# Cross-attention and routed experts on one core: a second norm with its own statistics, its first tile earlier, and weight splits in halves

## What is computed

```
def _layernorm(x, axis=-1, eps=1e-05):
    m = jnp.mean(x, axis=axis, keepdims=True)
    v = jnp.var(x, axis=axis, keepdims=True)
    return (x - m) / jnp.sqrt(v + eps)
...
        scores = jnp.einsum('bhqd,bhkd->bhqk', q, k) / jnp.sqrt(jnp.float32(D_K))
        scores = jnp.where(m == 0, jnp.float32(NEG_INF), scores)
        p_attn = jax.nn.softmax(scores, axis=-1)
        x = jnp.einsum('bhqk,bhkd->bhqd', p_attn, v)
        return jnp.einsum('bsd,ed->bse', x, Wo) + bo
...
        xa = xf @ P_w.T
        C1 = _route_combine_weights(xa, U1, K_ROUTE, TAU)   # top 3 of 12, softmax over them
        h = jax.nn.gelu(_mixture(xf, C1, W1), approximate=False)
        y = _mixture(h, C2, W2) + C3 @ b2
...
    x = x + _L0_xattn_ref(_layernorm(x, axis=-1), ctx_1024, ctx_1024, mask_BxSxS2_ik1, ...)
    x = x + _L0_ffn_ref(_layernorm(x, axis=-1), ...)
```

## Time and profile before

| | us |
|---|---|
| median of 3 runs | 414.63 |
| lowest, highest | 414.23, 415.75 |
| span of the profiled execution | 412.4 |

### The profile page before, as it was taken

How to read it: one execution, slowest core, us unless ns; L and a number is a source line. 1 busy time by engine, 2 the same in 40 slices (tenths; PEclk the granted TensorE clock), 3 DMA queues, 4 the chain that set the end, 5 groups by cost and what they waited for, 6 DMA issues and landing times.

```text
span 412.4 us, 7824 instructions
## 1 busy us (share of the span) xinstructions
PE 392.4 (95%) x2132; PEld 331.0 (80%) x2132; DVE 342.9 (83%) x1036; ACT 115.8 (28%) x263; POOL 110.9 (27%) x165
## 2 busy tenths in 40 slices
PE   4499999999989999999999999999999999999996
PEld 4388988989868888888888888888888888888884
DVE  3998889889885889789897988989789898888875
ACT  3477888888822111010110101011010100101000
POOL 5462755657520220202112020211202112020200
PEclk9999999999989999999999999999999999999999
DMA  7900123131000000000000000000000000000000
GB/s 225 333 2 2 61 92 98 55 102 51 2 0 3 0 2 13 13 0 13 0 13 13 0 13 0 13 0 13 13 0 13 0 13 13 0 13 0 14 0 26
DMA packets 8612, 12.71 MB, mean 31 GB/s; under 512 B 1076, under 2 KB 5016, under 8 KB 8472
## 3 DMA queue, kind: packets, MB, share of 16 engines
q1 hardware_dynamic: 8040, 12.44, 9.1%
q10 hardware_dynamic: 560, 0.13, 0.1%
HBM read 10.47 MB, written 2.10 MB: 30 GB/s over the span
## 4 chain that ended last, share of the span: by engine, by line
PE 89%; DVE 4%; issue 3%; ACT 2%; DMA 1%; POOL 1%; ACTq 0%; DVEq 0%; POOLq 0%
PE banks L920 68%; PE banks L997 5%; PE banks L987 3%; PE banks L962 3%; PE banks L972 2%; PE banks L975 2%; PE banks L977 2%; PE banks L1035 1%; DMA bk_sb<-in_bk_dram 1%; PE banks L1043 1%; DVE q_hl L625 1%; PE banks L1025 1%; PE banks L1008 1%; PE banks L953 1%; DVE s_max L631 1%
## 5 line engine op out<-in xcount | busy, mean ns | idle before, releaser
L815 DVE SCALAR_TENSOR_TENSOR s_d<-banks,c_cur,s_d 128x256 f32<-128x256 f32 x165 | 72.7, 478 | 27.6 <-PE banks L920 23.1
L920 PE MATMUL banks<-w_h,xf_h 128*128 128x512 f32 x204 | 81.8, 401 | 0.0
L920 PE MATMUL banks<-w_l,xf_h 128*128 128x512 f32 x204 | 80.6, 395 | 0.0
L920 PE MATMUL banks<-w_h,xf_l 128*128 128x512 f32 x204 | 80.2, 393 | 0.0
L406 POOL TENSOR_TENSOR top_e<-euler,top_d 128x9 f32<-128x9 f32 x16 | 28.9, 1807 | 185.1 <-DVE top_d L765 185.1
L920 PE MATMUL banks<-w_h,h_h 128*128 128x512 f32 x180 | 73.5, 408 | 0.0
L920 PE MATMUL banks<-w_l,h_h 128*128 128x512 f32 x180 | 71.1, 395 | 0.0
L920 PE MATMUL banks<-w_h,h_l 128*128 128x512 f32 x180 | 71.1, 395 | 0.0
L815 DVE SCALAR_TENSOR_TENSOR sum<-banks,c_new,sum 128x256 f32<-128x256 f32 x160 | 66.6, 476 | 3.2 <-PE banks L920 3.1
L561 ACT ACTIVATE h_h<-banks 128x256 fp32r<-128x256 f32 x15 | 5.8, 385 | 156.5 <-PE banks L1043 156.5
L920 PEld LDWEIGHTS banks<-w_l,xf_h 128*128 128x128 f32 x204 | 38.6, 189 | 8.5
(11 more groups left out here) (126 smaller groups left out, 618.5 us busy)
## 6 DMA issues: line engine op xcount, KB each, us to landing
stage<-in_w_t_dram SPq DMA_DIRECT2D x12, 512.0 KB, 3.7
out_dram<-x_all SPq DMA_DIRECT2D x16, 128.0 KB, 1.9
x_all<-in_x_dram SPq DMA_DIRECT2D x1, 1024.0 KB, 8.0
x_all<-in_x_dram SPq DMA_DIRECT2D x1, 768.0 KB, 7.9
mask_all<-in_mask_dram SPq DMA_DIRECT2D x2, 256.0 KB, 5.1
x_all<-in_x_dram SPq DMA_DIRECT2D x2, 128.0 KB, 3.5
wk_sb<-in_wk_t_dram SPq DMA_DIRECT2D x1, 256.0 KB, 3.7
wq_sb<-in_wq_t_dram SPq DMA_DIRECT2D x1, 256.0 KB, 4.3
```

What stands on the lines that cost most here:

```text
L815: dve.scalar_tensor_tensor(out=sums[e % 2][:, :], in0=product, scalar=weights[:, e:e + 1], in1=sums[e % 2][:, :], op0=ALU.mult, op1=ALU.ad ...
L920: ins = pe.matmul(dst, a(c), b(c), start=(i == 0), stop=(i == len(terms) - 1))
```

## The change

It has four parts.

1. The second norm gets tiles of its own: `bn2`, `mean_var2`, `var_eps2`, `rstd2`, and functions of its own on VectorE (`stats2`, `normalise2`) and GpSimd (`inverse_deviation2`).
2. Its first tile moves. On VectorE the statistics of tile 0 stand ahead of step T-4 = 12 and its normalisation right behind that step; statistics of tile 1 stand behind `xf_low(0)`. On GpSimd the inverse deviation of tile 0 stands ahead of the split of chunk 10 (it stood ahead of that of chunk 11).
3. ScalarE rounds `xf_h` from PSUM, not from `xf_t`, and waits neither for its own copy nor for `xf_low` of the tile before; VectorE's `xf_low` subtracts from PSUM as well. What overwrites `ps_t` waits for `xf_lo` where it waited for `xf_copied` (TensorE's `transpose_xf(1)`, `transpose_h`).
4. GpSimd splits each weight chunk in two instructions of 128x512.

```
             def split_weights(n, slot):
                 pool.wait_ge(w_hi, n + 1)
-                pool.tensor_tensor(w_l[:, n, :, :], stage[:, slot, :, :], w_h[:, n, :, :].bitcast(F32),
-                                   ALU.subtract).then_inc(w_split, 1)
+                for c in range(C):
+                    ins = pool.tensor_tensor(w_l[:, n, c, :], stage[:, slot, c, :], w_h[:, n, c, :].bitcast(F32),
+                                             ALU.subtract)
+                ins.then_inc(w_split, 1)
...
                     add_output_bias(T - 1)
-                    inverse_deviation(0, stats2_ready, var2_ready, rstd2_ready)
+                if n == CHUNKS - 2:
+                    inverse_deviation2(0)
                 split_weights(n, n % RING)
...
                 if later(t, 1):
                     act.wait_ge(z_done, t)
-                    act.wait_ge(xf_lo, t)
                 nc.scalar.activation(xf_t[:, :, :], ps_t, ACT.Copy).then_inc(xf_copied, 1)
-                act.wait_ge(xf_copied, t + 1)
-                nc.scalar.activation(xf_h[:, :, :], xf_t[:, :, :], ACT.Copy).then_inc(xf_hi, 1)
+                nc.scalar.activation(xf_h[:, :, :], ps_t, ACT.Copy).then_inc(xf_hi, 1)
...
+            stats2(0)
             attention(T - 4)
-            statistics(0, x_all, bn2_done, stats2_ready)
+            normalise2(0)
 
             def xf_low(t):
+                dve.wait_ge(xf_copied, t + 1)
                 dve.wait_ge(xf_hi, t + 1)
-                dve.tensor_tensor(xf_l[:, :, :], xf_t[:, :, :], xf_h[:, :, :].bitcast(F32), ALU.subtract).then_inc(xf_lo, 1)
+                dve.tensor_tensor(xf_l[:, :, :], ps_t, xf_h[:, :, :].bitcast(F32), ALU.subtract).then_inc(xf_lo, 1)
...
             a_low(T - 4)
-            normalise(0, x_all, xf, rstd2_ready, xf_ready)
             q_low(T - 1)
             divide_by_sum(T - 3)
             add_attention(T - 4)
-            statistics(1, x_all, bn2_done, stats2_ready)
             xf_low(0)
+            stats2(1)
...
                 pe.wait_ge(xf_ready, t + 1)
                 if later(t, 2):
                     pe.wait_ge(h_lo, t - 1)
+                elif t == 1:
+                    pe.wait_ge(xf_lo, 1)
                 else:
-                    pe.wait_ge(xf_copied if t else xt_copied, 1 if t else T)
+                    pe.wait_ge(xt_copied, T)
...
             def transpose_h(t):
                 pe.wait_ge(h_ready, t + 1)
                 n = min(t + 2, T) if isinstance(t, int) else t + 2
-                pe.wait_ge(xf_copied, n)
+                pe.wait_ge(xf_lo, n)
```

More of the change, by code:

```diff
@@ L132, in xattn_ffn_kernel @@
         rstd = sb("rstd", [P, 1])
+        bn2 = sb("bn2", [P, 6])
+        mean_var2 = sb("mean_var2", [P, 2])
+        var_eps2 = sb("var_eps2", [P, 1])
+        rstd2 = sb("rstd2", [P, 1])
         xn = sb("xn", [P, D])
@@ L350, in _, with inverse_deviation, inverse_deviation2 @@
             pool.wait_ge(consts_set, 16)
-            def inverse_deviation(t, stats, var, out_sem):
-                pool.wait_ge(stats, t + 1)
-                pool.tensor_tensor(var_eps[:, :], mean_var[:, 1:2], eps[:, :], ALU.add).then_inc(var, 1)
-                pool.wait_ge(var, t + 1)
-                pool.tensor_tensor(rstd[:, :], var_eps[:, :], minus_half[:, :], ALU.pow).then_inc(out_sem, 1)
+            def inverse_deviation(t):
+                pool.wait_ge(stats_ready, t + 1)
+                pool.tensor_tensor(var_eps[:, :], mean_var[:, 1:2], eps[:, :], ALU.add).then_inc(var_ready, 1)
+                pool.wait_ge(var_ready, t + 1)
+                pool.tensor_tensor(rstd[:, :], var_eps[:, :], minus_half[:, :], ALU.pow).then_inc(rstd_ready, 1)
+            def inverse_deviation2(t):
+                pool.wait_ge(stats2_ready, t + 1)
+                pool.tensor_tensor(var_eps2[:, :], mean_var2[:, 1:2], eps[:, :], ALU.add).then_inc(var2_ready, 1)
+                pool.wait_ge(var2_ready, t + 1)
+                pool.tensor_tensor(rstd2[:, :], var_eps2[:, :], minus_half[:, :], ALU.pow).then_inc(rstd2_ready, 1)
             def add_output_bias(t):
@@ L365, in split_weights @@
                 pool.wait_ge(w_hi, n + 1)
[L366 to L367 removed]
+                for c in range(C):
+                    ins = pool.tensor_tensor(w_l[:, n, c, :], stage[:, slot, c, :], w_h[:, n, c, :].bitcast(F32),
+                                             ALU.subtract)
+                ins.then_inc(w_split, 1)
             def attention(t):
[L370 removed]
+                inverse_deviation(t)
                 add_output_bias(t - 1)
[L373 to L374 removed]
+            inverse_deviation(0)
+            inverse_deviation(1)
             pool.wait_ge(setup_dve, 5)
             place_low_keys(pool, 0, kbd_set)
[L377 removed]
+            inverse_deviation(2)
             pool.wait_ge(bo_in, 16)
@@ L425, in _ @@
             exponentials(0)
-            inverse_deviation(1, stats2_ready, var2_ready, rstd2_ready)
+            inverse_deviation2(1)
             exponentials(1)
@@ L429, in _ @@
             with pool.Fori(2, T) as t:
-                inverse_deviation(t, stats2_ready, var2_ready, rstd2_ready)
+                inverse_deviation2(t)
                 exponentials(t)
@@ L592, in _, with statistics, stats2 @@
         def _(dve):
-            def statistics(t, src, done, ready):
-                dve.bn_stats(bn[:, :], src[:, t, :]).then_inc(done, 1)
+            def statistics(t, parts, dst, done, ready):
+                dve.bn_stats(parts[:, :], x_all[:, t, :]).then_inc(done, 1)
                 dve.wait_ge(done, t + 1)
                 dve.memset(waited[:, :], 0.0)
-                dve.bn_aggr(mean_var[:, :], bn[:, :]).then_inc(ready, 1)
-            def normalise(t, src, dst, rstd_sem, ready):
-                dve.wait_ge(rstd_sem, t + 1)
-                dve.tensor_scalar(dst[:, :], src[:, t, :], mean_var[:, 0:1], rstd[:, 0:1],
-                                  ALU.subtract, ALU.mult).then_inc(ready, 1)
+                dve.bn_aggr(dst[:, :], parts[:, :]).then_inc(ready, 1)
             def stats1(t):
-                statistics(t, x_all, bn_done, stats_ready)
+                statistics(t, bn, mean_var, bn_done, stats_ready)
+            def stats2(t):
+                statistics(t, bn2, mean_var2, bn2_done, stats2_ready)
             def normalise1(t):
@@ L610, in normalise1 @@
                     dve.wait_ge(xt_done, t)
-                normalise(t, x_all, xn, rstd_ready, xn_ready)
+                dve.wait_ge(rstd_ready, t + 1)
+                dve.tensor_scalar(xn[:, :], x_all[:, t, :], mean_var[:, 0:1], rstd[:, 0:1],
+                                  ALU.subtract, ALU.mult).then_inc(xn_ready, 1)
             def normalise2(t):
-                dve.wait_ge(xft_done, t)
-                normalise(t, x_all, xf, rstd2_ready, xf_ready)
+                if later(t, 1):
+                    dve.wait_ge(xft_done, t)
+                dve.wait_ge(rstd2_ready, t + 1)
+                dve.tensor_scalar(xf[:, :], x_all[:, t, :], mean_var2[:, 0:1], rstd2[:, 0:1],
+                                  ALU.subtract, ALU.mult).then_inc(xf_ready, 1)
             def q_low(t):
@@ L884, in experts @@
                 if ahead:
-                    statistics(t + 2, x_all, bn2_done, stats2_ready)
+                    stats2(t + 2)
                 layer1_pairs(t + 1, range(0, 3))
```

4 lines of the change are left out of this document (removed).

## The result

The changed kernel takes 416.11 us (median of 6, 415.68 to 417.49), the kernel before 414.43 beside it (6, 413.94 to 415.75): a ratio of 1.0043, 95% interval 1.0025 to 1.0060. I forecast 414.2 and a range up to 415.6; it is slower by 1.7 us, outside the range, and the sign of the difference is the other one. Of all the executions that follow, one (of e10_xf_256) took 664.26 us at a mean granted clock of 0.556; it is left out of that kernel's median and ratio.

The account below looks back on a forecast made before the run. TensorE was taken as the bound, full from 140 to 400 us, with only attention and the change of stages able to move. Halves +0.5 and low part -0.95 sum to -0.45 on 414.63: 414.2 us, range 412.3 to 415.6.

Parts of the forecast that it names:

- Parts worth nothing: Expert stage: rounding from PSUM and lower waits gain nothing beside a full TensorE; otherwise 0.07 us a tile.
- the one on the slower side (statistics blocked): Rival: GpSimd's splits block the moved `BN_STATS` and tile 1's statistics, giving 416.9 us; chance 0.06.
- Halves: Attention loop: half splits cost 0.10 us more a chunk, five on the chain, +0.5 us, bounds 0 and +1.0.
- Statistics moved: Tile 0's statistics, ahead of `max_scores(13)`, are nearly free: 0.1 us reaches scores(14), bounds 0 and 0.3.
- Normalisation moved: Tile 0's normalisation, moved earlier, removes the 0.41 us stall ahead of scores(15): -0.45 us.
- Low part from PSUM: Change of stages: `max_scores(15)`, `a_low(13)` and `output_project(13)` come earlier, -0.95 us, bounds -0.6 and -1.1.
- The working on the wait for `xf_h`: Change of stages: VectorE waits from about 110.9 to 112.03 us with nothing else listed, so early `q_low` gives nothing.
- an idle time of 1.06 us would still bring the fall at 118 us: Change of stages: 1.06 us idle ahead of `output_project(13)` leaves a clock window of 0.5 behind it.
- as a rival (0.22): Rival: shorter idle time ahead of `output_project(13)` keeps the clock full, a further -1.65 us, 412.5 us; chance 0.22.

Follow-up runs that it names:

- e10_xf_256: The kernel before with 256 bytes left free ahead of `xf_h`, the same place modulo 256: 414.21 us, ratio 0.9998.
- e1_pad_before: The kernel before with the four new tiles allotted behind `rstd` but unused, pushing later tiles 128 bytes further: 416.16 us, ratio 1.0042.
- e2_after_tail: The changed kernel with the four new tiles allotted behind all others, so `xn` to `h_l` lie as before: 413.83 us, ratio to before 0.9980.
- e6_pad_xf_only: The kernel before with only `xf_h` and `xf_l` 128 bytes further, all other tiles in place: 416.35 us, ratio 1.0044.
- e4_before_halves: The kernel before with only the weight splits done in two halves: 413.88 us, ratio 0.9976.
- e8_e3_stats_first: The changed kernel with new tiles allotted last, whole splits, and tile 1's statistics ahead of `xf_low(0)`: 410.94 us, ratio to before 0.9902.
- e7_before_psum: The kernel before with only `xf_h` rounded and `xf_l` subtracted from PSUM, with the waits that go with it: 411.16 us, ratio 0.9912.
- e15_xf_0: The kernel before with `xf_h` and `xf_l` moved to begin at a multiple of 256 bytes, `h_h` kept modulo 256: 416.76 us, ratio 1.0054.
- e17_after_aligned: The changed kernel with 128 bytes free ahead of `xf_h` and 96 ahead of `h_h`: 411.50 us, ratio to before 0.9925.
- e16_reorder_mended: e12_e8_reorder with `inverse_deviation2(0)` right behind the split of chunk 9 and 96 bytes free ahead of `h_h`: 408.30 us, ratio to before 0.9828.
- e12_e8_reorder: e8_e3_stats_first with GpSimd's loop order changed, the next step's inverse deviation ahead of the split: 412.28 us, ratio to before 0.9938.

## Why the prediction was wrong

**The step that failed** is the one under "Parts worth nothing", and the sentence ahead of it, that nothing in the change adds to or takes from TensorE's list in the expert stage. The list was indeed the same; I took 260.00 of 260.00 us busy to mean that its pace was given by the list, and so put the place of the four new tiles at nothing without a reason. It isn't: the pace of a split matmul was 0.2285 us in one layer and 0.2333 in the other already in the kernel before, side by side in one trace, and I didn't ask why. The four added tiles moved `xf_h`, and the first layer fell to the second's pace: 14 tiles x 0.107 = 1.5 us, shown by e1_pad_before (the tiles alone give the slowdown), e2_after_tail (with them out of the way the change gives 0.9980) and e6_pad_xf_only (`xf_h` and `xf_l` alone). No rival of mine had this either; the one on the slower side (statistics blocked) did not happen, `BN_STATS` took 0.43 us beside the split.

**Halves, +0.5 forecast, +0.94 measured** (0.97 in e4_before_halves), with high bound +1.0. A pair takes 2.53 to 2.55 us, not 2.50, and the next variance starts 2.49 us behind the split's start (88.51 to 91.00) where it was 2.34. That is 0.15 a chunk and not 0.10, and five of them are 0.75; the last 0.2 I can't explain, but it lies early: the first two of the nine steps take 13.37 us and not 12.82. I also had the halves as pure cost, and e4_before_halves shows their other side, the blocked subtraction down to 0.91 us, which in the change itself is worth nothing.

**Statistics moved, +0.1 forecast, +0.11 measured**, in part by luck: `normalise1(15)` was to shrink to 0.41 us and took 0.72, again ending with the bias addition beside it. **Normalisation moved, -0.45 forecast with that 0.1 in it, so -0.55 against scores(14); -0.55 measured**, and it decided nothing by itself (e8_e3_stats_first against e7_before_psum). **Low part from PSUM, -0.95 forecast;** `output_project(13)` comes 1.50 - 2.64 = -1.14 against scores(14), where the forecast was -1.05, and waits 0.99 us against 1.06. The duration was 0.42 against 0.41. These steps held, to 0.1 us. The working on the wait for `xf_h` missed one thing: "VectorE waits for that ... it has nothing else in its list" is true only as long as the statistics are put behind, and that order costs some 0.5 us (e8_e3_stats_first).

**The clock.** The forecast said that an idle time of 1.06 us would still bring the fall at 118 us, and as a rival (0.22) that it would not. In the profiled execution the clock was full there (1.00 from 100 to 140 us), so that rival's mechanism was right, but two stretches at lower clock had come in the first 40 us, and medians are about the sum of all. I can't tell from these runs what a single edit does to the clock. The 19 profiled executions lean one way without settling it. With an idle time of 1.54 to 1.57 us ahead of `output_project(13)` the clock fell behind it in 8 of 9 (not in e15_xf_0); with 0.98 to 1.00 us in 2 of 4, among them e17_after_aligned, which is the changed kernel but for two pads; with 0.46 or 0.47 us in 1 of 3 (e16_reorder_mended); with 0.39 or none in neither of two; and in e12_e8_reorder it fell behind the 1.60 us ahead of `output_project(12)`. So the missing fall in the changed kernel's profile is not a property of the change.

**The sum.** With the mis-sized and the missing term: +0.94 + 0.11 - 1.14 + 1.5 + 0.3 = +1.7 on 414.43: 416.1, as measured. The 0.3 behind the last logits holds the rest of the expert work and the last fall of the clock, and is not taken apart further.

## What to carry to other kernels

An engine that is busy 100% of a stage isn't thereby at its best pace: compare the spacing of like instructions within the stage and between kernels (here the count in a full window, 1201, 1194 and 1214). When a change allots a tile, note what it pushes, and try the stationary and the moving tiles of the heavy matmuls at the same place modulo 256 bytes; 96 bytes of padding were worth more here (-3.4 us) than any order of the edits. Test each part alone before they are joined: one of four parts held the gain, and the halves only shorten a collision that another part removes. And compare several executions before reading a fall of the clock as the work of an edit.

## What the hardware showed that I had not expected

The start-to-start time of a matmul of split operands with 512 columns depends on where its stationary tile lies in SBUF relative to the moving one: 0.227 to 0.229 us where both begin at the same place modulo 256 bytes, 0.232 to 0.234 where the stationary tile lies 64, 128 or -32 bytes further in the first layer, and 160, 32 or -96 in the second. The durations in the records hardly tell (0.39 and 0.40 us). What in the chip does it is open: loads of the stationary tile and reads of the moving one run beside each other, and a conflict between them would fit, but no run here separates that from other causes. The Trainium skill ("SBUF — State Buffer", Who interferes with whom) gives the two kinds of read ports of their own and has TensorE wait on nobody; by that rule e6_pad_xf_only should have taken the time of the kernel before, and it took 2.1 us more than that kernel beside it. The measurement decides.

Nor did I expect that a normalisation with a single SBUF tensor, started 0.07 us too late, takes 2.47 us and not 0.41, with an idle time of 1.60 us of TensorE and a stretch at half clock behind it (e12_e8_reorder).
